# Second attention: the place of the weighted values in the slot with the output projection

## What is computed

```python
q = decoder_output @ wq_w + wq_b
k = encoder_output @ wk_w + wk_b
v = encoder_output @ wv_w + wv_b
...
score = jnp.einsum('bhqd,bhkd->bhqk', q, k) / jnp.sqrt(jnp.asarray(KEY_SIZE, dtype=jnp.float32))
score = score * mask
score = jnp.where(score == 0, jnp.float32(NEG_INF), score)
alignment = jax.nn.softmax(score, axis=-1)
context = jnp.einsum('bhqk,bhkd->bhqd', alignment, v)
...
heads = context @ wo_w + wo_b
```

## Time and profile before

| | us |
|---|---|
| median of 3 runs | 1593.97 |
| range of the runs | 1591.99 to 1598.27 |
| profiled execution | 1596.73 |
| its span, first to last instruction | 1594.9 |
| PE busy | 1407.7 (88%) |
| DVE busy | 1224.6 (77%) |
| ACT busy | 1104.7 (69%) |
| mean granted clock of TensorE | 0.942 |

### The profile page before, as it was taken

How to read it: one execution, slowest core, us unless ns; L and a number is a source line. 1 busy time by engine, 2 the same in 40 slices (tenths; PEclk the granted TensorE clock), 3 DMA queues, 4 the chain that set the end, 5 groups by cost and what they waited for, 6 DMA issues and landing times. The chain is left out here.

```text
span 1594.9 us, 40553 instructions
## 1 busy us (share of the span) xinstructions
PE 1407.7 (88%) x15436; PEld 998.3 (63%) x15436; DVE 1224.6 (77%) x3127; ACT 1104.7 (69%) x2444; POOL 176.1 (11%) x237
## 2 busy tenths in 40 slices
PE   5899999999999998780778888898989799999996
PEld 3567676666666666430756665666656567788884
DVE  5889888888888888479669999898989676344443
ACT  4777777777777776486349888888888544366663
POOL 1000000001100000000000000000000310034443
PEclk8999999999999999895779999999999589999998
DMA  7133232333233220000021212110100162222221
GB/s 209 44 99 97 86 97 87 99 104 103 87 110 106 77 67 21 1 1 27 1 64 51 82 45 88 45 61 19 36 19 12 35 243 69 60 35 48 45 46 24
DMA packets 65230, 105.69 MB, mean 66 GB/s; under 512 B 7497, under 2 KB 39474, under 8 KB 63890
## 3 DMA queue, kind: packets, MB, share of 16 engines
q1 hardware_dynamic: 58322, 94.83, 18.9%
q0 software_dynamic: 6720, 8.27, 3.2%
HBM read 68.88 MB, written 35.11 MB: 65 GB/s over the span
## 5 line engine op out<-in xcount | busy, mean ns | idle before, releaser
L1443 ACT ACTIVATE a_p<-a_s,a_nb 112x375 f32<-112x375 f32 x256 | 140.9, 598 | 26.3 <-DVE a_nb L1556 25.4
L1363 PE MATMUL a_ps_t<-ident,a_p 112*128 112x112 f32 x768 | 119.8, 287 | 42.4 <-ACT a_p L1443 41.3
L554 ACT ACTIVATE a_p<-a_ps_s,a_nb 112x375 f32<-112x375 f32 x256 | 144.1, 572 | 15.9 <-DVE a_scaled L714 15.4
L134 PE MATMUL a_ps_o<-a_vh,a_pt 125*128 125x64 f16 (+1 forms) x1536 | 153.0, 183 | 2.1 <-ACT a_pt L1456 0.8
L136 PE MATMUL a_ps_o<-a_vh,a_pt 125*128 125x64 f16 (+1 forms) x1536 | 151.3, 182 | 0.0
L135 PE MATMUL a_ps_o<-a_vl,a_pt 125*128 125x64 f16 (+1 forms) x1536 | 151.1, 182 | 0.0
L1363 PEld LDWEIGHTS a_ps_t<-ident,a_p 112*128 112x128 f32 x768 | 81.5, 148 | 98.6 <-issue 83.6
L134 PEld LDWEIGHTS a_ps_o<-a_vh,a_pt 125*128 125x128 f16 x1536 | 133.9, 98 | 13.1 <-ACT a_pt L1456 4.9
L135 PEld LDWEIGHTS a_ps_o<-a_vl,a_pt 125*128 125x128 f16 x1536 | 131.1, 98 | 11.1
L1556 DVE CUSTOM_DVE_ANT_0 a_s<-a_s,a_fill 112x375 f32<-112x375 f32 x256 | 130.3, 547 | 5.5
L2232 ACT ACTIVATE e_h<-e_p,tile_b 128x128 f32<-128x128 f32 x280 | 86.7, 366 | 68.5 <-PE e_p L136 68.4
(11 more groups left out here) (445 smaller groups left out, 4505.4 us busy)
## 6 DMA issues: line engine op xcount, KB each, us to landing
a_piece<-in_w SPq DMA_DIRECT2D x72, 256.0 KB, 3.0
split_weights<-a_pair SPq DMA_DIRECT2D x72, 256.0 KB, 3.3
w<-split_weights SPq DMA_DIRECT2D x8, 1024.0 KB, 6.2
a_ctx<-in_ctxT SPq DMA_DIRECT2D x16, 375.0 KB, 3.7
ctx<-a_cx SPq DMA_DIRECT2D x16, 375.0 KB, 4.7
a_cx<-ctx SPq DMA_DIRECT2D x16, 375.0 KB, 6.0
w1h<-split_weights SPq DMA_DIRECT2D x2, 1792.0 KB, 13.9
w1l<-split_weights SPq DMA_DIRECT2D x2, 1792.0 KB, 16.3
```

What stands on the lines that cost most here:

```text
L134: nc.tensor.matmul(out, wh, mh, start=(i == 0), stop=False)
L554: nc.scalar.activation(p32[:, g % 2, i, 0:NC], ps_s[0:S, i, 0:NC], ACT.Exp, bias=nb[:, g % 2, i:i + 1], scale=SC, accum_out=rsum[:, h:h + ...
L1363: mm = nc.tensor.matmul(ps_t[:, 2 * (g % 2) + i, t * S:(t + 1) * S], p32[:, g % 2, i, t * KV:t * KV + 128], ident32[0:S, 0:S], start=(t == ...
L1443: nc.scalar.activation(p32[:, g % 2, i, 0:NC], s2[:, g % 2, i, :], ACT.Exp, bias=nb[:, g % 2, i:i + 1], scale=-1.0).then_inc(exp_done, 1)
```

## The change

In the slots with p = 3, where the job is W, PE takes `weighted_values(g - 2)` behind the scores and ahead of the transposes. In all other slots it stays behind the job. The programs of the other engines are as before, and so are all waits. The condition holds in 16 slots, g = 3, 11, ..., 123, the one of batch 0 among them, where the job is V1.

```diff
             for g in range(SLOTS):
                 if g < G:
                     scores(g)
+                behind_output = g % NP == JOBS.index(("W", -1))
+                if behind_output and g - 2 < G:
+                    weighted_values(g - 2)
                 if 0 <= g - 1 < G:
                     transposes(g - 1)
                 for name, b in slot_job(g):
                     job(name, b)
-                if 0 <= g - 2 < G:
+                if not behind_output and 0 <= g - 2 < G:
                     weighted_values(g - 2)
                 if 0 <= g - 1 < G:
                     take_high(g - 1)
```

## The result

| | us |
|---|---|
| before, median of 4 runs | 1594.12 |
| changed, median of 4 runs | 1633.90 (1632.70 to 1636.83) |
| ratio, 95% interval | 1.0261 (1.0243 to 1.0280) |
| profiled execution, its span | 1636.83, 1635.1 |
| mean granted clock of TensorE | 0.917 |

By the medians the kernel is slower by 39.8 us, 2.5% (the ratio in the table is 1.0261). The forecast was slower by 19.9, with 1631 as the upper end of the range. The direction and the wait were right, the size was half of what came.

A forecast was written before the change was run, and what follows sets the result against it. No engine is full; the loop through PE, DVE and ACT bounds the stage. Order 14.0, batches 0 and 15 1.4 and clock 4.5 sum to +19.9 us on the median 1593.97: 1613.9 us, range 1600 to 1631.

The forecast's parts named there:

- The late low part: Slot 3: moved weighted values wait for the low part ACT makes behind exponentials(2), starting at 2.46 us, ahead of the transposes.
- The price at full clock: Slot 3 of batches 1 to 14: the new order delays each batch by 1.0 us, +14.0 us in all.
- The count of drops: Batches 1 to 14: TensorE's clock falls to half in 11 batches, bounds 8 to 14, against 8 before.
- Batches 0 and 15: First and last batch, with fewer or no exponential waits: 0.7 us each, between 0 and 0.9, +1.4 us together.
- What a drop costs: Slot 3 at half clock: 1.2 us for each drop in the new order, against 1.09 before.
- 13.2 - 8.7: Clock term for batches 1 to 14: 11 drops at 1.2 us less the 8 existing at 1.09, +4.5 us.
- Rival 2: Clock stays low for a second stretch, through scores(4) and transposes(3), drops in all 14 batches: +37.5 us, 1631; chance 0.18.
- The drops did not vanish: Rival for slot 3: the low-clock stretches disappear after the move, +6.7 us, 1600.7; chance 0.09.
- the shift was not swallowed: Rival behind slot 3: the batch's later waits absorb the delay and 8 drops are gained, 1585 us; chance 0.04.
- the move was not free: Rival for slot 3: low part already there when scores end, so the swap does nothing, 1594 to 1599; chance 0.05.
- The rule of the Trainium skill: Slot 3: only idle gaps longer than any here lose clock, so no drops; sum without drops +15.4 us.

The follow-up runs named there:

- before, both slots filled: Kernel before plus unused filler matmuls of 240 columns, 7 in slot 3 and 13 in slot 5 of each batch: 1587.74 us, ratio 0.9952.
- changed, both slots filled: Changed kernel plus unused filler matmuls of 240 columns, 17 in slot 3 and 13 in slot 5: 1601.56 us, ratio 1.0041.
- the early low part: Changed kernel with ACT making the low part of the probabilities ahead of the exponentials in slots with p = 2: 1593.77 us, ratio 1.0020.
- the wait alone: Kernel before, order kept, with PE waiting for the low part of slot g - 2 ahead of the transposes where p = 3: 1628.26 us, ratio 1.0216.

## Why the prediction was wrong, point by point

**The account.** From the residual update of batch 1 to that of batch 14, thirteen batches:

| kernel | us | against filled |
|---|---|---|
| before, both slots filled | 346.43 | |
| before | 353.92 | +7.49 |
| changed, both slots filled | 358.82 | |
| changed | 392.23 | +33.41 |

The order costs 358.82 - 346.43 = 12.39 us, 0.95 a batch. The clock costs 7.49 us before and 33.41 after, 25.92 more. Together 38.31, nearly all of the 39.8 measured. That the filler takes the clock's part away and nothing else rests on the full-clock batches, which are as long with it as without (26.45 and 27.41).

**The late low part: right.** The values wait for ACT, and ACT makes the low part behind the exponentials: 2.46 was worked out for their start and 2.46 came (1140.39 to 1142.85). This is shown by the early low part, which removes the wait, and by the wait alone, which brings it back without the move.

**The price at full clock: right.** 1.0 us a batch was taken, between 0.87 and 1.09; 0.97 came. Next scores 4.91 for 4.98, high part 1144.12 and 1146.71, that is 3.73 and 6.32, for 3.81 and 6.24 to 6.46. The 0.95 by which the second high part is later than before (6.32 against 5.37) goes through to the end of the batch whole, and DVE's 0.55 is the part that is swallowed, as said.

**The count of drops: about right.** Ten of fourteen; eleven were taken.

**Batches 0 and 15: too small.** 1.4 us was taken for both. From the first scores of batch 0 to those of batch 1 the trace has 31.44 us before (818.10 to 849.54) and 33.74 after (817.51 to 851.25), 2.3 more, and the slots of batch 15 up to the scores of its last are 0.7 longer. Part of that is clock as well.

**What a drop costs: wrong, and this is the step that failed.** I took 1.2 us for one, because the stretches of the kernel before lasted 3.41 us and I priced slot 3 with one such stretch in it. In the changed kernel they last 6.8 to 20.5 us, and the cost of one is 33.41 / 10 = 3.3 us. For slot 3 the price was sound: where the stretch begins in the pause, as in batch 6, the next scores come 6.06 us behind the slot's start, and 6.04 was worked out. What was missing is what follows. Against the changed kernel with both slots filled, the starts of the scores in batches 1 to 14 put 18.9 of the 33.4 us into slot 4 (4.53 us in place of 2.64, ten times), 7.3 into slot 5, 5.5 into slot 3 and about 2 into slot 6. Behind slot 3 I had allowed 1.2 less 1.06, 0.14 a drop. With the measured costs of the clock the term "13.2 - 8.7" is 33.4 - 7.5 = 25.9 where 4.5 stood, and the sum becomes 41.

Rival 2, a second stretch in every batch at 1631 with a chance of 0.18, had this mechanism. It came near in time (+37.5) by two errors that nearly cancel: it took 14 drops at 2.2 us, and there were 10 at 3.3, eight of them with stretches longer than twice 3.41 us. The sign for it in the trace, batch 15 at half clock for several slots, stood in the prediction as an argument for that rival, but went neither into the term nor into the range of the forecast.

**The other rivals.** The drops did not vanish (1600.7), the shift was not swallowed (1585), and the move was not free (1594 to 1599).

**The range.** It ended at the central value of rival 2, as if that value had no error of its own. A rival with 0.18 has to have its own range inside.

**The rule of the Trainium skill.** The page "TensorE: Matmul & The Clock Gate", section "Why this matters for your kernels", puts the loss of clock down to idle gaps between bursts that are longer than any here. By it there would be no drops, and 1609. The runs don't agree: the pauses in slot 3 are 1.81 us in the changed kernel, and filling them with work that nothing needs takes out most of the stretches. What holds is the direction of the rule, that idle time on PE costs clock.

**What stays open.** Why a stretch ends after 3.4 us in one batch and after 20.5 in another was not settled. Filling slot 5 alone made most of them short but left four long; that slots at half clock are light by themselves and so keep it low is argued, not shown. Nor do the runs tell in which batches a stretch begins: batches 10, 11, 13 and 14 of the changed kernel have the same slots as 9 and 12 and keep full clock, and the wait alone, with a pause of the same length in slot 3, drops in five batches and not in ten. Each kernel has one trace, so how these counts vary from execution to execution is not known either.

## What to carry to other kernels

Before work is moved into an idle gap, look where the gap's engine would wait for its operands, on the releasing engine's own queue: here the operand came 1.8 us behind the start of the gap, and the wait without the moved work made most of the loss. In a loop that already loses TensorE's clock now and then, a microsecond more of idle time in one slot can bring drops that cost 3.3 us each, most of it in slots that the change doesn't touch; price a drop by how long it may last, and give that its own bounds. A pair of kernels with cheap filler matmuls in the pauses separates the price of an order from that of the clock in one comparison.

## What the hardware showed that was not expected

- TensorE's granted clock stayed at 0.50 for up to 20.48 us inside a loop in which PE was busy 18.89 us of that time.
- Useless matmuls made the kernel before faster: 13 + 7 of 240 columns in each batch took it from 1595.29 to 1587.74 us (0.9952, 0.9920 to 0.9984). Seven in slot 3 alone did nothing, since the stretches moved to slot 5.
- The same pause of 1.45 us was followed by full clock in one kernel, and in six of fourteen batches by half clock in another that differed in seven matmuls in an earlier slot.
